# First conditioned product ahead of the third merge group, its weights made in halves, x loaded by SyncE

## The chip, the cores and the metric

The kernel runs on one core of one Trainium2 chip. The metric is device time in microseconds of one execution, lower is better. Engines in this text: PE (TensorE), ACT (ScalarE), DVE (VectorE), POOL (GpSimd), SP (SyncE, which only issues DMAs here). Each takes its own instructions in order, and they wait for each other by semaphores.

## What is computed

The input x has 8 batches of 256 tokens of width 128 (2048 tokens). Two layers follow each other, each a conditioning step and a feed-forward network:

```python
# layer 0: conditioning, a two-layer net whose weights depend on the batch's id
hidden_i = x @ wi.T + 2 * (x @ common_wi_a.T) @ common_wi_b.T + expert_lora(x, ids, ...)
hidden_o = relu(hidden_i) @ wo.T + 2 * (...)          # the same low-rank terms for wo
# layer 0: mixture of 4 experts, top 2 by a gate, 4 rounds with residual
for r in range(4):
    logits = cur @ Wg[r] + bg[r]; top 2, softmax -> cw
    y = gelu(cur @ W1[e] + b1[e]) @ W2[e] + b2[e]      # all 4 experts
    cur = cur + sum_e cw[e] * y[e]
x = x + cur
# layer 1: language low-rank projection, then a gated net of ternary weights
x = x + ffn1(lora(x, language) + embedding)
```

`wi` is 512x128 and `wo` 128x512. With the low-rank terms added, each batch has its own two weight matrices of 128x512; the kernel calls them (b, 0) for the first and (b, 1) for the second.

## The kernel before

The tokens lie on the free axis in four chunks of 512 columns, two batches to a chunk, and the 128 features on the partitions. Every product of 32-bit numbers is made of three matmuls on parts rounded to fp32r: `product` (L503) multiplies the high part of the weights with the high part of x (L505) and with its low part (L506), and the low part of the weights with the high part of x (L509). So every operand is first split: a high part is a rounding copy, mostly on ACT, and a low part is operand minus high part, on DVE or POOL.

The change touches only the stretch ahead of the loop over the expert rounds. What happens there:

- **Loads.** SP issues ids, vectors, factors of batch 0, 2, 4, 5, 6, 7 (`first_load`, `lora_load`, `expert_load` at L247), then the expert weights `moe_w` in four loads of 512 KB into `cw_all` (`moe_raw`), then small language factors. ACT issues `cond_base` (wi and wo), chunk 0 of x, and the factors of batches 1 and 3. POOL issues chunks 1 to 3 of x (L413).
- **Merge groups** (`merge_group`, L511). Low-rank factors are multiplied into PSUM banks, seven groups in the order of `MERGE_GROUPS`: (b, 0) by one 512-column matmul (L524), (b, 1) by four of 128 columns (L527). `MERGE_BANKS` names the bank of each; a group waits until the sums out of its banks are done.
- **Sums, high and low parts of the merged weights.** DVE adds the base (`merged_sum`, L1025) in the order `SUMS`, ACT rounds (`merged_high`, L798, into `mer_hi`, shown as ffn_hi) in the order `HIGHS`, POOL subtracts (`merged_low`, L417, into `mer_lo`, shown as ffn_lo) in the order `LOWS`; only (0, 0) has its low part on DVE (`first_low`, L1030). Six buffers hold the sums, four batches the parts.
- **x.** `x0_high` (ACT, L876) and `x0_low` (DVE for chunks 0, 2, 3, POOL for 1) split the chunks.
- **cond_hidden(b)** (L552) is the first conditioned product of a batch, 4 x 3 matmuls of 256 columns; `relu_high` (ACT, L871) and `relu_low` (DVE, L1209) split its result. **cond_out(b)** (L572) is the second one, 12 matmuls into bank COND. After two batches `conditioned_high` and `conditioned_copy` (ACT, L880, L885) and `conditioned_low` (DVE, L1043) take the chunk out; the next cond_out waits for that.
- **moe_high** (ACT, L890) and **moe_low** (POOL, L428) split the expert weights piece by piece, the first gate and the first expert of the first chunk are begun (`expert_in`, four pieces), `merge_lang` (L540) makes the language weights, and the loop over the rounds begins.

`warm` (L587) issues matmuls of zeros: 13 at the start and `KEEP_WARM` = 2 behind the second merge group. The order on each engine is written out by hand, on PE in L673 to L706:

```python
            merge_group(0)
            merge_group(1)
            warm(KEEP_WARM)
            merge_group(2)
            merge_group(3)
            cond_hidden(0)
            cond_hidden(1)
            merge_group(4)
            cond_out(0)
```

In the text the groups are counted from one: the third group is `merge_group(2)`.

## Time and profile before

| what | us |
|---|---|
| median of 3 runs | 485.58 (485.28 to 486.13) |
| profiled execution, device time | 486.61 |
| its span, first to last instruction | 484.8 |
| PE busy | 477.9 (99%) |
| ACT busy | 393.9 (81%) |
| DVE busy | 387.7 (80%) |
| POOL busy | 118.7 (24%) |

The span is 1.8 us shorter than the profiled execution's own time, and that execution is 1.0 us above the median of the runs. A page row of a busy engine says nothing yet about where time is lost; for that one asks for the waits of the engine that is nearly always busy, and for its instructions in order of time. The stretch ahead of the loop is the first 45 us of the span.

### The profile page before, as it was taken

To read this page: it belongs to the slowest core of one execution; us is meant where nothing else is said; L and a number is where in the kernel's file an instruction comes from. 1 tells how busy PE (TensorE), PEld (TensorE's weight loads), DVE (VectorE), ACT (ScalarE), POOL (GpSimd) and SP (SyncE) were. 2 spreads that over 40 slices of the span, in tenths; PEclk is the share of its full clock that TensorE was granted. 3 is DMA by queue.
4 is the path that set the end of the run, shared out by engine and by line. 5 is a ranking of instruction groups with operands and counts; after the bars stand their busy time and mean duration, and the time that the engine had idled before them with its cause. 6 is when DMAs were issued, how large, how long until landed. Compare 5 with 4: busy or idle time off the path is not lost.

```text
span 484.8 us, 7478 instructions
## 1 busy us (share of the span) xinstructions
PE 477.9 (99%) x2270; PEld 397.0 (82%) x2270; DVE 387.7 (80%) x641; ACT 393.9 (81%) x542; POOL 118.7 (24%) x102
## 2 busy tenths in 40 slices
PE   7999999999999999999999999999999999999997
PEld 7998888888888888888888888888888887888885
DVE  4789899999879898988898898889897758554343
ACT  3799988888888888988888888888888888697653
POOL 5796212121212112121222121231313144400000
PEclk9999999999999999999999999999999999999999
DMA  7702702020201102020202012120202000000001
GB/s 209 215 5 88 266 18 89 2 87 3 87 11 76 71 16 87 0 87 0 87 0 87 11 76 82 49 89 0 87 2 87 2 0 0 1 0 1 0 22 69
DMA packets 6986, 26.30 MB, mean 54 GB/s; under 512 B 2226, under 2 KB 2610, under 8 KB 4786
## 3 DMA queue, kind: packets, MB, share of 16 engines
q1 hardware_dynamic: 5826, 21.20, 12.1%
q0 software_dynamic: 528, 3.67, 2.2%
q10 hardware_dynamic: 608, 1.11, 0.8%
q8 instruction: 14, 0.23, 0.2%
q14 instruction: 10, 0.08, 0.0%
HBM read 24.81 MB, written 1.18 MB: 54 GB/s over the span
## 4 chain that ended last, share of the span: by engine, by line
PE 96%; DMA 2%; SPq 1%; issue 0%; DVE 0%
PE bank L505 34%; PE bank L506 34%; PE bank L509 26%; DMA stage<-lora_all 2%; PE bank L594 1%; PE bank L595 1%; PE bank L527 1%; SPq L244 0%; SPq L247 0%; PE bank L540 0%; PE bank L524 0%; SPq L257 0%; DVE x L1276 0%; SPq L345 0%; SPq L344 0%
## 5 line engine op out<-in xcount | busy, mean ns | idle before, releaser
L812 ACT ACTIVATE act_out<-bank,vec 128x512 f32<-128x512 f32 x256 | 165.4, 682 | 41.8 <-PE bank L509 32.6
L1115 DVE TENSOR_TENSOR hid_lo<-act_out,hid_hi 128x1024 fp32r<-128x1024 f32 x128 | 156.6, 1243 | 33.3 <-ACT hid_hi L817 33.2
L817 ACT ACTIVATE hid_hi<-act_out 128x1024 fp32r<-128x1024 f32 x128 | 135.9, 1062 | 8.0 <-PE bank L509 0.2
L468 POOL TENSOR_TENSOR cur<-cur,prod 128x512 f32<-128x512 f32 x48 | 64.9, 1352 | 238.4 <-DVE prod L1126 237.9
L505 PE MATMUL bank<-hid_hi,moe_hi 128*128 128x512 f32 x256 | 99.9, 390 | 0.0
L509 PE MATMUL bank<-hid_hi,moe_lo 128*128 128x512 f32 x256 | 99.7, 390 | 0.0
L505 PE MATMUL bank<-xhi,moe_hi 128*128 128x512 f32 x256 | 99.7, 390 | 0.0
L506 PE MATMUL bank<-hid_lo,moe_hi 128*128 128x512 f32 x256 | 99.7, 389 | 0.0
L506 PE MATMUL bank<-xlo,moe_hi 128*128 128x512 f32 x256 | 99.6, 389 | 0.0
L509 PE MATMUL bank<-xhi,moe_lo 128*128 128x512 f32 x256 | 99.6, 389 | 0.0
L505 PEld LDWEIGHTS bank<-hid_hi,moe_hi 128*128 128x128 f32 x256 | 48.1, 188 | 11.3 <-issue 0.2
L509 PEld LDWEIGHTS bank<-hid_hi,moe_lo 128*128 128x128 f32 x256 | 48.1, 188 | 10.2
L506 PEld LDWEIGHTS bank<-hid_lo,moe_hi 128*128 128x128 f32 x256 | 48.1, 188 | 10.1
L509 PEld LDWEIGHTS bank<-xhi,moe_lo 128*128 128x128 f32 x256 | 48.1, 188 | 10.0
L505 PEld LDWEIGHTS bank<-xhi,moe_hi 128*128 128x128 f32 x256 | 48.0, 188 | 10.0
L506 PEld LDWEIGHTS bank<-xlo,moe_hi 128*128 128x128 f32 x256 | 48.1, 188 | 9.9
L1126 DVE SCALAR_TENSOR_TENSOR prod<-bank,vec,cw_all 128x512 f32<-128x512 f32 x64 | 47.5, 742 | 0.2 <-PE bank L509 0.2
L505 PE MATMUL bank<-hid_hi,ffn_hi 128*128 128x512 f32 (+1 forms) x108 | 37.8, 353 | 0.0
L506 PE MATMUL bank<-hid_lo,ffn_hi 128*128 128x512 f32 (+1 forms) x108 | 37.4, 350 | 0.0
L999 ACT ACTIVATE act_out<-bank,vec 128x512 f32<-128x512 f32 x32 | 21.3, 685 | 14.5 <-PE bank L506 14.3
L505 PE MATMUL bank<-xhi,ffn_hi 128*128 128x512 f32 (+1 forms) x84 | 30.4, 362 | 0.0
L506 PE MATMUL bank<-xlo,ffn_hi 128*128 128x512 f32 (+1 forms) x84 | 30.0, 357 | 0.0
(126 smaller groups left out, 569.9 us busy)
## 6 DMA issues: line engine op xcount, KB each, us to landing
cw_all<-cw_dram SPq DMA_DIRECT2D x16, 1024.0 KB, 4.6
stage<-ffn_w POOLq DMA_DIRECT2D x1, 2304.0 KB, 8.5
cw_all<-moe_w SPq DMA_DIRECT2D x4, 512.0 KB, 10.3
stage<-lora_all SPq DMA_DIRECT2D x5, 160.0 KB, 7.1
x<-x_t POOLq DMA_DIRECT2D x3, 256.0 KB, 7.0
out_t<-x SPq DMA_DIRECT2D x3, 256.0 KB, 2.5
cur<-cond_base ACTq DMA_DIRECT2D x2, 256.0 KB, 3.1
stage<-ffn_w POOLq DMA_DIRECT2D x1, 512.0 KB, 3.8
```

What stands on the lines that cost most here:

```text
L468: pool.tensor_tensor(cur[:, c, :], cur[:, c, :], prod[:, s % 2, :], ALU.add).then_inc(add_done, 1)
L505: pe.matmul(out, w_hi, r_hi, start=start, stop=False)
L506: mm = pe.matmul(out, w_hi, r_lo, start=False, stop=stop and w_lo is None)
L509: return pe.matmul(out, w_lo, r_hi, start=False, stop=stop)
L527: mm = pe.matmul(bank[:, at, fc * D:(fc + 1) * D], factors[:, fc * P:(fc + 1) * P], factors[:, F:F + D], start=True, stop=True)
L594: pe.matmul(bank[0:SQ, at, :], wg_now[:], xhi[:, c, :], start=True, stop=False)
L595: pe.matmul(bank[0:SQ, at, :], wg_now[:], xlo[:, c, :], start=False, stop=True).then_inc(logit_done, 1)
L812: act.activation(act_out[:, f // 2, f % 2, :], bank[:, f, :], ACT.Gelu_apprx_tanh, bias=vec[:, V_B1 + e * FC + f:V_B1 + e * FC + f + 1]).t ...
L817: act.activation(hid_hi[:, s % 2, 2 * pr:2 * pr + 2, :], act_out[:, pr, :, :], ACT.Copy)\
L999: act.activation(act_out[:, o // 2, o % 2, :], bank[:, o + FC * (at % 2), :], ACT.Gelu, scale=vec[:, v + o:v + o + 1]).then_inc(gelu_done, 1)
L1115: dve.tensor_tensor(hid_lo[:, s % 2, 2 * pr:2 * pr + 2, :], act_out[:, pr, :, :], hid_hi[:, s % 2, 2 * pr:2 * pr + 2, :].bitcast(F32), ALU ...
L1126: dve.scalar_tensor_tensor(prod[:, s % 2, :], bank[:, 4 + s % 2, :], vec[:, V_B2 + e:V_B2 + e + 1], cw_all[:, c % 2, e, :], ALU.add, ALU.m ...
```

## The change

On PE, cond_hidden(0) moves from behind the fourth merge group to directly behind the second one and its warming matmuls, of which there are now three. The weights (0, 0) that it needs are summed, rounded and subtracted in two halves of 256 columns (`first_sum`, `first_merged_high`, `first_low`), with semaphores of their own, and PE waits for the second half before the third piece of the product. The third and fourth group write banks 6, 7, 4, 5 instead of 2, 3, 6, 7. Chunks 1 to 3 of x are issued by SP: chunk 1 behind the factors of batch 2, chunks 2 and 3 behind those of batch 7 and ahead of the expert weights. x0_low(2) and the low parts of conditioned chunks 2 and 3 go from DVE to POOL, where the latter read the copy in `cur` instead of the bank, so that cond_out(6) waits for the copy alone. The split of the gate weights goes from DVE to POOL. The orders of sums, high and low parts, and the lists of ACT, DVE and POOL up to the loop are rewritten; cond_hidden(4) moves behind cond_out(2).

```diff
-MERGE_BANKS = (6, 7, 4, 5, 2, 3, 6, 7, 5, 6, 7, 5, 6, 7, 5, 6)
+MERGE_BANKS = (6, 7, 4, 5, 6, 7, 4, 5, 5, 6, 7, 5, 6, 7, 5, 6)
-WARM, KEEP_WARM = 13, 2
+WARM, KEEP_WARM = 13, 3
...
             expert_load(sp, 2, expert)
+            x_load(sp, 1)
             for b in (4, 5, 6, 7):
                 lora_load(sp, b)
+            x_load(sp, 2)
+            x_load(sp, 3)
...
-            pool.wait_ge(first_out_in[1], 16)
-            for c in range(1, CHUNKS):
-                x_load(pool, c)
...
+            def conditioned_low(c):
+                pool.wait_ge(cond_cur, c + 1)
+                pool.tensor_tensor(xlo[:, c, :], cur[:, c, :], xhi[:, c, :].bitcast(F32), ALU.subtract)\
+                    .then_inc(xs_done, 1)
...
+            split_gate()
             merged_low(1, 0)
             merged_low(0, 1)
+            merged_low(1, 1)
             x0_low(1)
-            merged_low(1, 1)
...
                 for f in range(FC):
+                    if b == 0 and f % 2 == 0:
+                        pe.wait_ge(first_lo_done, f // 2 + 1)
...
+                elif b == PER_CHUNK * (CHUNKS - 1):
+                    pe.wait_ge(cond_cur, c)
...
             warm(KEEP_WARM)
+            cond_hidden(0)
             merge_group(2)
             merge_group(3)
-            cond_hidden(0)
...
-            cond_hidden(4)
             merge_group(6)
             cond_out(2)
+            cond_hidden(4)
             cond_out(3)
...
+            def first_merged_high():
+
+                for half, summed, done in zip(halves, (first_sum_done, merge_free), (first_hi_done, mer_hi_done)):
+                    act.wait_ge(summed, 1)
+                    act.activation(mer_hi[:, 0, 0, half], merged(0, 0)[:, half], ACT.Copy).then_inc(done, 1)
...
             base_load(act, 1)
+            x0_high(0)
             lora_load(act, 3)
-            x0_high(0)
-            merged_high(0, 0)
+            first_merged_high()
...
+            def first_sum():
+
+                dve.wait_ge(base_in[0], 16)
+                dve.wait_ge(merge_done, MERGED.index((0, 0)) + 1)
+                for half, summed in zip(halves, (first_sum_done, merge_free)):
+                    dve.scalar_tensor_tensor(merged(0, 0)[:, half], bank[:, merge_bank(MERGED.index((0, 0))), half], COND_ALPHA,
+                                             base[:, 0, half], ALU.mult, ALU.add).then_inc(summed, 1)
...
-            split_gate()
             x0_low(0)
-            merged_sum(0, 0)
+            first_sum()
+            first_low()
             merged_sum(1, 0)
             merged_sum(0, 1)
-            first_low()
```

On ACT, between the first relu and the first conditioned step, before. ffn_hi is a high part of merged weights, `hid_hi<-bank` a relu, `xhi<-x` a chunk of x, `xhi<-bank` the conditioned chunk's high part, `moe_hi` an expert piece.

```order
L871 ACTIVATE hid_hi<-bank 128x1024
L798 ACTIVATE ffn_hi<-stage 128x512
L798 ACTIVATE ffn_hi<-act_out 128x512
L876 ACTIVATE xhi<-x 128x512
L871 ACTIVATE hid_hi<-bank 128x1024
L798 ACTIVATE ffn_hi<-stage 128x512
L880 ACTIVATE xhi<-bank 128x512
L876 ACTIVATE xhi<-x 128x512
L885 ACTIVATE cur<-bank 128x512
L890 ACTIVATE moe_hi<-cw_all 128x512
```

The same place after the change, from the second relu to the copy of the conditioned chunk.

```order
L903 ACTIVATE hid_hi<-bank 128x1024
L922 ACTIVATE moe_hi<-cw_all 128x512
L824 ACTIVATE ffn_hi<-fifth 128x512
L908 ACTIVATE xhi<-x 128x512
L903 ACTIVATE hid_hi<-bank 128x1024
L824 ACTIVATE ffn_hi<-stage 128x512 x2
L912 ACTIVATE xhi<-bank 128x512
L917 ACTIVATE cur<-bank 128x512
```

The first expert piece stood behind the first conditioned chunk's copy and now stands ahead of it, behind relu_high(1).

On SP, from the factors of batch 7 on, before: the expert weights follow at once.

```order
L244 TENSOR_LOAD ids
L244 ISA x2
L247 ISA
L247 DMA stage<-lora_all 64x640
L355 DMA cw_all<-moe_w 128x1024 x4
```

And after, with the last two chunks of x between them (chunk 1 stands in the same way behind the factors of batch 2).

```order
L247 TENSOR_LOAD ids
L247 ISA x2
L250 ISA
L250 DMA stage<-lora_all 64x640
L265 DMA x<-x_t 128x512 x2
L361 DMA cw_all<-moe_w 128x1024 x4
```

Three x loads, one of them further ahead, now stand before the first load of expert weights.

## Rows read from the trace of the kernel before

**Rows 1.** The page, part 1: busy us (share) and instructions.

```profile
PE 477.9 (99%) x2270; PEld 397.0 (82%) x2270; DVE 387.7 (80%) x641; ACT 393.9 (81%) x542; POOL 118.7 (24%) x102
```

**Rows 2.** Waits of PE, whole span: us in total, times, longest.

```profile
PE bank L524 <- DMA stage<-lora_all: 2.3, 2, 1.8
```

**Rows 3.** PE in order of time: start, us, instruction [idle before, releaser].

```profile
9.53 0.70 PE L524 MATMUL bank<-stage 32*128 32x512 f32 x2 [1.78 <-DMA stage<-lora_all]
...
10.74 0.38 PE L505 MATMUL bank<-xhi,ffn_hi 128*128 128x256 f32 x1
...
15.90 0.70 PE L524 MATMUL bank<-stage 32*128 32x512 f32 x2 [0.53 <-DMA stage<-lora_all]
...
17.00 0.38 PE L505 MATMUL bank<-hid_hi,ffn_hi 128*128 128x256 f32 x1
...
22.68 0.28 PE L505 MATMUL bank<-xhi,ffn_hi 128*128 128x256 f32 x1
...
24.12 0.28 PE L505 MATMUL bank<-xhi,ffn_hi 128*128 128x256 f32 x1
...
26.74 0.38 PE L505 MATMUL bank<-hid_hi,ffn_hi 128*128 128x256 f32 x1
...
44.02 0.50 PE L505 MATMUL bank<-xhi,moe_hi 128*128 128x512 f32 x1
```

**Rows 4.** Three stretches: us, busy by engine, PE clock, DMA share, GB/s.

```profile
7.67:11.08 3.41, 1.62 (x23) 1.46 (x23) 2.74 (x5) 2.42 (x4) 2.29 (x3) 1.00 0.82 236
11.08:14.49 3.41, 3.41 (x19) 3.41 (x18) 2.06 (x4) 1.68 (x3) 1.81 (x2) 0.50 1.03 263
14.49:17.90 3.41, 2.88 (x26) 2.58 (x26) 2.10 (x3) 2.59 (x5) 2.63 (x3) 1.00 1.03 336
```

**Rows 5.** DVE in order of time: first sums, first low part, a 256-column operation.

```profile
6.91 1.29 DVE L1025 SCALAR_TENSOR_TENSOR prod<-bank,cur 128x512 f32<-128x512 f32 x2
...
8.71 0.68 DVE L1030 TENSOR_TENSOR ffn_lo<-prod,ffn_hi 128x512 fp32r<-128x512 f32 x1
...
34.28 0.41 DVE L1065 TENSOR_TENSOR bank<-bank,logit 32x256 f32<-32x256 f32 x1
```

**Rows 6.** ACT in order of time: an expert piece, a relu, a high part.

```profile
24.38 0.63 ACT L890 ACTIVATE moe_hi<-cw_all 128x512 fp32r<-128x512 f32 x1
24.90 1.02 ACT L871 ACTIVATE hid_hi<-bank 128x1024 fp32r<-128x1024 f32 x1
25.80 0.64 ACT L798 ACTIVATE ffn_hi<-fifth 128x512 fp32r<-128x512 f32 x1
```

**Rows 7.** SP's issues in order of time.

```profile
4.75 5.55 SPq L247 DMA_DIRECT2D stage<-lora_all  x5
10.34 2.21 SPq L355 DMA_DIRECT2D cw_all<-moe_w  x4
```

**Rows 8.** DMA issues near 1.2, 4.7, 5.8, 10.3: size, us to landing.

```profile
x<-x_t ACTq DMA_DIRECT2D x1, 256.0 KB, 3.2
...
stage<-lora_all SPq DMA_DIRECT2D x1, 160.0 KB, 3.8
...
x<-x_t POOLq DMA_DIRECT2D x1, 256.0 KB, 6.8
...
cw_all<-moe_w SPq DMA_DIRECT2D x1, 512.0 KB, 9.1
stage<-lora_all SPq DMA_DIRECT2D x1, 160.0 KB, 7.1
```

**Rows 9.** Stretches of 2 us, columns as in rows 4.

```profile
12.00:14.00 2.00, 2.00 (x11) 2.00 (x11) 1.14 (x2) 1.19 (x2) 0.64 (x1) 0.50 1.03 233
...
16.00:18.00 2.00, 2.00 (x20) 1.88 (x21) 0.97 (x2) 1.18 (x3) 1.12 (x1) 1.00 1.01 381
...
20.00:22.00 2.00, 2.00 (x21) 1.82 (x20) 1.61 (x3) 1.54 (x2) 2.00 (x3) 1.00 0.32 75
```

**Rows 10.** POOL in order of time: six expert low parts.

```profile
36.61 7.55 POOL L428 TENSOR_TENSOR moe_lo<-cw_all,moe_hi 128x512 fp32r<-128x512 f32 x6
```

More of the change, by code:

```diff
@@ L454, in _ @@
             moe_low(3)
+            conditioned_low(2)
+            pool.wait_ge(cond_cur, CHUNKS)
+            for i in range(2):
+                pool.memset(prod[:, i, 0:1], 0.0).then_inc(add_done, 1)
             moe_low(7)
+            conditioned_low(3)
             def mixture_add(rnd, s, last):
@@ L929, in _ @@
             merged_high(5, 1)
+            relu_high(5)
+            merged_high(7, 1)
             merged_high(6, 1)
[L931 to L935 removed]
+            moe_high(6)
             relu_high(6)
+            moe_high(3)
             conditioned_high(2)
```

130 lines of the change are left out of this document (61 added, 69 removed).

## The prediction

> **What bounds the kernel now.** I read the page's busy times first, then the waits of the tensor engine, then its order of time with the clock of each stretch, and last what feeds that stretch. The tensor engine (PE) is busy for 477.9 of 484.8 us [rows 1], and over the whole span, once it has begun, it waits only for low-rank factors that a DMA brings: twice, 2.3 us in total, 1.8 us of it before the third merge group at 9.53 [rows 2, 3]. After 15.90 it never waits for another engine again. One more loss is no wait: the granted clock is 0.50 (1.2 GHz) from 11.08 to 14.49, after a stretch in which PE was busy 1.62 of 3.41 us, and 1.00 (2.4 GHz) before and after [rows 4]. The first conditioned product, whose 12 matmuls take 1.44 us at the full clock (22.68 to 24.12, the same block for batch 3), lies in that stretch. So all that the change can win lies ahead of 16 us: 2.3 us of waits and about 1.6 us of slow clock, 3.9 us together; from 16 us on PE has only to be kept fed. A gain there reaches the end one for one, since PE works without a wait from there.
>
> **The first product, moved ahead of groups 3 and 4.** Today the row at 10.74 is cond_hidden(0) [rows 3]. Its weights are a chain: the sum on VectorE (DVE) from 6.91, the high part on ScalarE (ACT), the low part on DVE from 8.71, 0.68 us [rows 5], and two other sums stand between. After the change the chain is made in halves with nothing between. A half has 256 columns; its price on each engine lies between the 0.41 us of a 32x256 operation and the 0.68 us of the whole [rows 5]; I take 0.41, since length along the row is what both have in common, for each of three steps. The first half is summed from 6.9 as now, and 6.9 + 3 x 0.41 + 0.1 for handovers gives 8.2: the first product starts 2.5 us earlier. Even at 0.68 each it starts at 9.0. The second half follows 0.3 us later and PE needs it 0.7 us later, so it costs nothing. The third warming matmul fills time in which PE would stand still. If the clock holds, the product ends at 9.7, groups 3 and 4 follow (1.21 us today, 9.53 to 10.74) and are now held by the sums of group 2, because their banks are 6, 7, 4, 5 again: three more sums at the 0.6 us at which sums follow each other come behind the halves, so (1,1) is done at 10.3 and the groups end at about 11.1, not 10.9: 0.2 us, which the wait before cond_out(0) would take anyway. Their own factors, of batch 3 above all, are issued 0.6 us later by ACT, behind x0_high(0); today the wait for them ends at 9.53, so they are due at 10.1 at the latest, 0.4 us after the product; I count 0.1, since x is not yet under way on a second queue.
>
> **Up to cond_out(2).** cond_hidden(1) ends near 12.7. The fifth group's factors (batch 5) are issued at 7.9, 0.55 later than now; today that wait ends at 15.90, some 8.5 us after the issue, while the first factors of this size from SP land after 3.8 us [rows 8]: 11.7 to 16.4. I take 12 to 13, because x chunks 2 and 3 are no longer ahead of them; past 14 each us would be lost. The group then ends near 13.9. cond_out(0) needs the low part of the first hidden block. relu_high(0) now stands behind x0_high(1) and the high part of (2,0), whose sum waits for group 3 and ends at 11.5: it starts at 12.1, takes 1.0, and after sums (2,0), (3,1), (3,0), (2,1), ending at 13.2, DVE's relu_low(0) ends at 14.4. So cond_out(0) starts at 14.6; today it starts at 17.00. Four products at 1.44 to 1.5 and two merge groups at the 1.10 us of 15.90 to 17.00 follow, 8.1 us: PE could start cond_out(2) at 22.7. Today it starts it at 26.74, after one product more (cond_hidden(4), 1.44). This is the floor.
>
> **What is late next: the expert weights.** cond_out(2) overwrites the bank that the first conditioned chunk sits in, so it waits for conditioned_low(0) on DVE, which waits for two ACT steps. ACT takes its work in order, and its new list has moe_high(0) ahead of merged_high(4,0), x0_high(3), relu_high(2), merged_high(4,1), merged_high(5,0) and those two steps. moe_high(0) waits for the first piece of moe_w. Call its landing M. From M: six 512-column steps at 0.52 (24.38 to 24.90), one relu at 0.90 (24.90 to 25.80) make 4.0 us up to and with the first conditioned step, the copy 0.6 (a step alone takes 0.63), the DVE low part 0.68, handovers 0.2 [rows 6]: cond_out(2) cannot start before M + 5.47. From there to the last block ahead of the loop (expert_in piece 3, at 44.02) PE needs today's 44.02 - 26.74 = 17.28 us and the 1.44 us of cond_hidden(4), which now stands behind. So that block starts at **M + 24.19**, and the break-even with today is M = 19.83.
>
> **Where M lands.** Today the first moe load is issued at 10.34 and lands 9.1 us later, at 19.4; the factors of batch 7, issued ahead of it at 9.8 (the last of the five), land after 7.1 us, at 16.9 [rows 7, 8]. Moving x from GpSimd's queue (POOL) to SyncE's (SP) puts three more issues ahead of the moe loads, 0.55 us each as the moe loads' own are (2.21 for four): the first moe issue moves to 12.0. Upper bound: the same 9.1 us from issue, M = 21.1. Lower bound: x chunk 3, issued at 11.45, lands in the 3.2 us of the first x load, 14.65, and 0.52 MB follow at 381 GB/s in 1.4 us, M = 16.0. Between them: the four factor loads and three x loads are 1.44 MB, which at the mixed stretch's 233 GB/s [rows 9] from 8.5 (4.75 + 3.8, when the load ahead of them has landed) end at 14.7; SP issues factors only every 1.27 us (five in 5.55) while 0.16 MB take 0.7, so its queue runs dry for perhaps 0.8 in all, 15.5; and today moe lands 2.5 us after the last load ahead of it. **M = 18.0.** I take this since it uses how the same queue behaves at the same place. The last block then starts at 42.19 against 44.02, 1.83 us earlier. Its own x landings: chunk 1 is issued at 5.35 and lands between 8.55 (3.2 us) and 12.15 (6.8, today's time on the other queue) [rows 8]; it delays relu_high(0) from 10.4 on, and I take 9.5, since it has only one factor load ahead. Chunk 2 (10.9, between 14.1 and 17.7) holds relu_high(1) and would decide from 15.2 on; I take 14.6.
>
> **POOL and DVE.** POOL gets x0_low(2) and conditioned_low(2), (3), three operations like those of its moe_lo row, six in 7.55 us [rows 10]: 3 x 1.26 = 3.8 us, and the small gate split before 6 us, when it idles. It loses the three x issues. Today its last low part ends at 44.2. After, low parts that PE needs come in time: merged_low(7,1), the tightest, ends at about 37.5 and cond_out(7) wants it at 38.9. POOL then ends near 45.4, and only loads and additions that the loop wants after 50 wait for it. Cost 0, and the cover is 1.4 us thick; beyond that every us counts. conditioned_low from DVE saves it 2 x 0.68 where it was not late. Other edits cost nothing: PE's second wait inside the first product is met as shown, and logits for chunk 1 ahead of cond_out(5), and the products of chunk 3 exchanged with pieces of the first expert, are the same matmuls in another order.
>
> **Sum** against the profiled execution: 486.61 (span 484.8 and 1.8 around it) less 1.83 is 484.8. The same difference taken from the median of the runs, 485.58, gives 483.75, so **483.8**.
>
> **Rivals.**
>
> (a) The DMA engines are the bound and the order of issue changes nothing. They are at 1.03 of full share from 12 to 14 and 1.01 from 16 to 18 [rows 9], and the bytes ahead of the first moe piece are the same in both kernels. Then M stays 19.4: the last block at 43.6, 0.4 us saved, 485.1. Against it: in the mixed stretch they move 233 GB/s at the share at which they move 381 later, so the share is not bytes. A late x chunk 1 (12.15, which gives 1.75 us back) or late factors of batch 5 (16.4) end close to it and are counted here.
>
> (b) The last load's tail goes away. After 20 us the engines are at 0.32 of their share, 75 GB/s [rows 9], though moe is still landing: a few of the 16 lag. If GpSimd's x loads cause that, moe follows x chunk 3 evenly, M is 16.9, and the floor of 22.7 decides: 22.7 + 18.72 = 41.4, 2.6 saved, 483.0. The Trainium skill (DMA: Bandwidth & Descriptors, section "Latency and other measured facts") says that two of the sixteen are usually slower and guesses that the descriptor rings of GpSimd's queue cause it; the trace shows the lag, not its cause.
>
> (c) The clock falls again. Instead of one pause of 1.8 us there are several: about 0.3 at 8, 0.2 at 12.7, 0.6 at 13.9, 0.8 at 22.7. Today a pause of 0.5 us left the clock at 1.00 (14.49 to 17.90, PE busy 2.88 of 3.41), one of 1.8 us brought 0.50 [rows 4]. A stretch at 0.50 costs up to 1.6 us, some of it inside pauses; I count 1.4: 485.2. The Trainium skill (TensorE: Matmul & The Clock Gate, section "A second HAM failure mode: psum-queue depth-cycling") warns of just this, short pauses between groups of matmuls that cycle through PSUM banks, which speaks against four groups on four banks; by that rule this case, with 485.2, would be the likeliest, by the row of the 0.5 us pause it is not.
>
> (d) Slower. The moe loads keep their 9.1 us from issue because SP's single queue is what delays them, and now it also carries x. M = 21.1, last block at 45.3, 1.3 later: **486.9**. It is slower than before from M = 19.8, measurably from 20.8.
>
> **How the numbers follow.** Forecast (M from 17 to 18.8, no slow stretch): 0.40; (a) 0.24; (b) 0.12; (c) 0.12; (d) 0.12. About 0.2%, 0.97 us, is what a measurement can tell here. Faster by more: the forecast and (b), 0.52; within: (a) and (c), 0.36; slower: (d), 0.12. The range goes from the floor with 0.1 to spare, 482.9, to 486.2: it takes in the forecast, (a), (b), (c) and the half of (d) with M up to 20.5.
>
> **What would show it.** First product at 8.2 to 8.6 in the order of time; no wait of PE for a DMA; a wait of about 0.8 us before cond_out(2), put down to DVE's conditioned low part, and before it ACT waiting for cw_all<-moe_w until 18; clock 1.00 from 7.67 to the end; last block at 42.2. I am wrong if ACT waits for moe_w to 19.4 or beyond, if a window shows 0.50, if cond_out or cond_hidden waits on POOL's ffn_lo, or if the loop, which nothing here touches, takes longer than now.

## The result, and the profile after the change

The changed kernel takes 487.24 us (median of 14 executions, 486.05 to 489.12) against 485.38 us (14 executions, 484.39 to 486.28) of the kernel before, measured on one chip. The ratio is 1.0045, with a 95% interval of 1.0034 to 1.0056. The kernel is slower by 0.45%; the forecast was 483.8 with a range of 482.9 to 486.2, and the measured time lies above it.

The profiled execution took 487.13 us, its span is 485.3. The page's busy times, which answer [rows 1]:

```profile
PE 477.5 (98%) x2272; PEld 395.9 (82%) x2272; DVE 387.4 (80%) x636; ACT 394.0 (81%) x543; POOL 121.0 (25%) x106
```

PE does the same work. What changed is where it waits. Waits of PE over the whole span, after (engine, bank and line, released by: total us, times, longest), to be held against [rows 2]:

```profile
PE bank L529 <- DVE xlo L1084: 1.7, 1, 1.7
PE bank L616 <- POOL blank L408: 1.1, 1, 1.1
PE bank L529 <- issue: 0.6, 1, 0.6
PE bank L548 <- DMA stage<-lora_all: 0.5, 2, 0.3
PE bank L529 <- DVE ffn_lo L1071: 0.2, 1, 0.2
```

The 2.3 us for factors [rows 2] have shrunk to 0.5. (The 1.1 us is the start, before anything can run.) In their place stand 1.7 us for DVE's low part of the first conditioned chunk and 0.8 us in two other places. PE in order of time, after, with the columns of [rows 3]:

```profile
8.95 0.36 PE L529 MATMUL bank<-xhi,ffn_hi 128*128 128x256 f32 x1 [0.20 <-DVE ffn_lo L1071]
...
10.84 0.70 PE L548 MATMUL bank<-stage 32*128 32x512 f32 x2 [0.23 <-DMA stage<-lora_all]
...
15.69 0.36 PE L529 MATMUL bank<-hid_hi,ffn_hi 128*128 128x256 f32 x1 [0.61 <-issue]
...
25.70 0.36 PE L529 MATMUL bank<-hid_hi,ffn_hi 128*128 128x256 f32 x1 [1.66 <-DVE xlo L1084]
...
44.31 0.50 PE L529 MATMUL bank<-xhi,moe_hi 128*128 128x512 f32 x1
```

These are the first product, the third group, cond_out(0), cond_out(2) and the last block ahead of the loop. That block starts at 44.31, and 44.02 before [rows 3], though the stretch at half clock of [rows 4] is absent. Who holds cond_out(2) is seen on ACT, after:

```profile
20.17 0.63 ACT L922 ACTIVATE moe_hi<-cw_all 128x512 fp32r<-128x512 f32 x1 [2.75 <-DMA cw_all<-moe_w]
20.71 0.62 ACT L824 ACTIVATE ffn_hi<-fifth 128x512 fp32r<-128x512 f32 x1
21.23 0.61 ACT L908 ACTIVATE xhi<-x 128x512 fp32r<-128x512 f32 x1
21.75 1.01 ACT L903 ACTIVATE hid_hi<-bank 128x1024 fp32r<-128x1024 f32 x1
22.66 1.14 ACT L824 ACTIVATE ffn_hi<-stage 128x512 fp32r<-128x512 f32 x2
23.69 0.58 ACT L912 ACTIVATE xhi<-bank 128x512 fp32r<-128x512 f32 x1
24.17 0.59 ACT L917 ACTIVATE cur<-bank 128x512 f32<-128x512 f32 x1
```

ACT stands still for 2.75 us until the first piece of expert weights is there. Then it works through six steps and the copy without a gap; DVE takes the low part at 24.87, and PE goes on at 25.70. SP's issue of those weights, to be held against [rows 7], and its size and time to landing, against [rows 8]:

```profile
12.02 2.72 SPq L361 DMA_DIRECT2D cw_all<-moe_w  x4
```

```profile
cw_all<-moe_w SPq DMA_DIRECT2D x1, 512.0 KB, 8.1
```

12.02 + 8.1 is 20.1: this is M, forecast at 18.0. The stretches of 2 us that answer [rows 9] (us, busy by engine, PE clock, DMA share, GB/s):

```profile
12.00:14.00 2.00, 1.86 (x19) 1.57 (x15) 2.00 (x4) 1.30 (x2) 2.00 (x2) 1.00 0.70 171
14.00:16.00 2.00, 1.39 (x15) 1.23 (x15) 2.00 (x3) 1.91 (x5) 2.00 (x3) 1.00 0.91 237
16.00:18.00 2.00, 2.00 (x19) 2.00 (x18) 1.95 (x4) 1.43 (x2) 2.00 (x3) 1.00 0.98 229
18.00:20.00 2.00, 2.00 (x20) 1.75 (x19) 0.76 (x2) 0.00 (x0) 2.00 (x2) 1.00 1.01 377
```

From 12 to 14 the DMA engines are at 0.70 of their share and move 171 GB/s, where before they were at 1.03 and 233 [rows 9]. From 16 to 18 their share is 0.98, but they move 229 GB/s where they moved 381 before; 377 comes only after 18. Everything from 45 us on is as it was: PE is busy without a gap from 45 to 400 in both kernels.

The clock needs one more look. In the profiled execution it is 1.00 throughout the first 45 us. But each timed execution lists its mean granted clock, and in 6 of these 14 it is 0.996, in the others 0.999 or 1.000. One stretch of 3.41 us at 0.50, as in [rows 4], lowers the mean over 485 us by 0.5 x 3.41 / 485 = 0.0035, about this much. The 6 took 488.04 to 489.12, the other 8 took 486.05 to 487.34. The execution of the kernel before from which the prediction was made was itself one at 0.996 (486.61 us), and such executions are rare in that kernel: 2 of the 119 timed in the experiments below. So at full clock the changed kernel needs 486.98 (median of the 8) and the kernel before about 485.2; the rest, 0.26 us of the median, comes with the clock.

### The profile page after: what moved, and what is told of

Its sections match the earlier page's. It is cut to its first block, busy times and chain, and to the rows that moved or that the text cites. A ratio compares the mean times of both kernels' runs of the same rounds, so it can differ in the third digit from the quotient of the medians.

```text
span 485.3 us, 7483 instructions
## 1 busy us (share of the span) xinstructions
PE 477.5 (98%) x2272; PEld 395.9 (82%) x2272; DVE 387.4 (80%) x636; ACT 394.0 (81%) x543; POOL 121.0 (25%) x106
## 4 chain that ended last, share of the span: by engine, by line
PE 94%; SPq 2%; DMA 2%; ACT 1%; issue 1%; DVE 0%; ACTq 0%; DVEq 0%
PE bank L529 34%; PE bank L530 33%; PE bank L533 25%; DMA cw_all<-moe_w 2%; PE bank L620 1%; PE bank L621 1%; SPq L247 1%; SPq L250 1%; SPq L265 0%; ACT ffn_hi L824 0%; PE bank L564 0%; ACT hid_hi L903 0%; SPq L260 0%; DVE xlo L1084 0%; ACT cur L917 0%
## 5 line engine op out<-in xcount | busy, mean ns | idle before, releaser
L844 ACT ACTIVATE act_out<-bank,vec 128x512 f32<-128x512 f32 x256 | 165.3, 682 | 42.7 <-PE bank L533 33.7
L1156 DVE TENSOR_TENSOR hid_lo<-act_out,hid_hi 128x1024 fp32r<-128x1024 f32 x128 | 158.8, 1260 | 31.9 <-ACT hid_hi L849 31.8
```

The source lines that it names most:

```text
L844: act.activation(act_out[:, f // 2, f % 2, :], bank[:, f, :], ACT.Gelu_apprx_tanh, bias=vec[:, V_B1 + e * FC + f:V_B1 + e * FC + f + 1]).t ...
L1156: dve.tensor_tensor(hid_lo[:, s % 2, 2 * pr:2 * pr + 2, :], act_out[:, pr, :, :], hid_hi[:, s % 2, 2 * pr:2 * pr + 2, :].bitcast(F32), ALU ...
```

## Experiments

Several things are new at once: the place of moe_high(0) on ACT's list, the x loads on SP's queue with the later expert weights, and the early first product with its lists and banks. My theory after the profile was that the first two together cost the time, because the list meets a load that is not there; the rivals were that the early product, x on SP alone, or the new lists cost it. The first four kernels were compared on one chip with 485.05 us (27 executions) of the kernel before.

**The changed kernel again**, for a second profile.

> The changed kernel itself, as the measure for the others on the same chip. Theory A (the first load of expert weights lands at 20.1 and ACT's list makes all wait for it): ratio to before near 1.0045, PE waits about 1.7 us for DVE's conditioned low part before cond_out(2), last block ahead of the loop near 44.3. Theory B (the clock decides: the changed kernel falls to 0.50 in some executions and then costs 1.5 us more): runs with a mean clock of 1.000 near 486.7, runs with 0.996 near 488.5, and the median between them depends on how many of each there are.

487.14 us (6 executions), ratio 1.0045 [1.0029, 1.0061]. The picture repeats: M is 20.05, cond_out(2) at 25.58 after a wait for the same low part. What differs is the start: the first merge group begins at 6.81 and not at 6.23, and the first product 0.58 later too:

```profile
9.53 0.36 PE L529 MATMUL bank<-xhi,ffn_hi 128*128 128x256 f32 x1 [0.68 <-DVE ffn_lo L1071]
...
25.58 0.36 PE L529 MATMUL bank<-hid_hi,ffn_hi 128*128 128x256 f32 x1 [1.23 <-DVE xlo L1084]
```

The start-up's 0.58 us is taken back by a shorter wait before cond_out(2), since that wait ends with M. Two of the 6 executions show a mean clock of 0.996, and they are the longest (488.13 and 488.16); the other four have a median of 486.83.

**moe_high(0) later.** The one edit is the place on ACT's list.

```diff
             relu_high(1)
-            moe_high(0)
             merged_high(4, 0)
...
             conditioned_copy(0)
+            moe_high(0)
             moe_high(4)
```

> One edit in the changed kernel: on ACT, moe_high(0) stands behind conditioned_copy(0), as it did before the change, instead of behind relu_high(1). Theory A: ACT no longer waits for cw_all<-moe_w before the first conditioned chunk, the wait of PE before cond_out(2) goes from 1.7 us to at most 0.2, the last block starts near 42.6, and the median falls by 1.7 us, to 485.5, ratio 1.000. Theory B: the wait goes, but the time still falls in two groups 1.5 us apart; a median of 486.5 or more would speak for B. A rival to both, that the engines have simply more to do in this order: the wait moves to cond_out(4) or to the low parts and the median stays at 487.2.

485.87 us (12 executions), ratio 1.0014 [1.0004, 1.0025]. 1.3 us come back, about six tenths of the loss. The weights land at 19.8 (12.03 + 7.8), but nobody waits. PE's waits up to 46 us in this kernel, beside the start:

```profile
PE bank L529 <- issue: 0.6, 1, 0.6
PE bank L548 <- DMA stage<-lora_all: 0.4, 1, 0.4
PE bank L529 <- DVE ffn_lo L1071: 0.2, 1, 0.2
```

The 1.7 us are gone, and so are the executions at 0.996: none of these 12, none of 10 in the repetition below, against 8 of 20 of the changed kernel. So about 1.0 of the 1.3 us is the wait (486.83 less 485.87), and the rest comes with the clock. cond_out(2) and the last block ahead of the loop start at:

```profile
23.83 0.38 PE L529 MATMUL bank<-hid_hi,ffn_hi 128*128 128x256 f32 x1
...
42.46 0.50 PE L529 MATMUL bank<-xhi,moe_hi 128*128 128x512 f32 x1
```

No wait stands before this cond_out(2). 23.83 is where PE itself comes to it; the prediction's floor had 22.7.

**The load earlier instead.** The place stays, the first load of expert weights is issued ahead of x chunks 2 and 3.

```diff
-            x_load(sp, 2)
-            x_load(sp, 3)
             for i in (0, 2, 1, 3):
                 half = slice((i % 2) * 2 * F, (i % 2 + 1) * 2 * F)
                 sp.dma_start(moe_raw[:, i // 2, half], moe_w[:, i // 2, half]).then_inc(moe_in[i], 16)
+                if i == 0:
+                    x_load(sp, 2)
+                    x_load(sp, 3)
```

> One edit in the changed kernel: SP issues the first load of expert weights ahead of x chunks 2 and 3, not behind them. Theory A with its formula (last block at landing + 24.2): the first load is issued at 10.9 instead of 12.0 and has 512 KB less ahead of it, so it lands near 18 and the last block would start near 42.4 by it; but x chunk 2 lands about 1.5 us later (near 17), and relu_high(1) stands behind it, which gives 43.5 to 44.0 (landing + 27). Median 486.0 to 486.7. If the landing does not move (DMA engines full, order of issue without effect), the time stays at 487.2.

485.95 us (10 executions), ratio 1.0021 [1.0011, 1.0031]. The first piece is issued at 10.92 and lands 4.2 us later, at 15.1, and moe_high(0) runs at 18.64, directly behind relu_high(1), without waiting:

```profile
18.64 0.62 ACT L923 ACTIVATE moe_hi<-cw_all 128x512 fp32r<-128x512 f32 x1
```

```profile
cw_all<-moe_w SPq DMA_DIRECT2D x1, 512.0 KB, 4.2
```

Its last block starts at 43.27, after waits of 0.68, 0.31 and 0.61 us ahead of 17. Two independent ways of taking away the meeting of place and landing give the same 1.2 to 1.3 us. That the meeting costs this much, with the clock that comes with it, is shown. That neither comes back to 485.1 shows that there is a second, smaller cost.

**The early first product alone**, in the kernel before: cond_hidden(0) ahead of the third group, the weights in halves, three warming matmuls; banks, loads and all other lists as before.

```diff
-WARM, KEEP_WARM = 13, 2
+WARM, KEEP_WARM = 13, 3
...
             warm(KEEP_WARM)
+            cond_hidden(0)
             merge_group(2)
             merge_group(3)
-            cond_hidden(0)
...
-            merged_sum(0, 0)
+            first_sum()
+            first_low()
             merged_sum(1, 0)
             merged_sum(0, 1)
-            first_low()
```

> The kernel before with one part of the change alone: cond_hidden(0) directly behind the second merge group, its weights made in halves, three warming matmuls; loads, banks and all other orders as before. Theory A: what ends the first 16 us is the landing of batch 5's factors (15.75), not the product before it and not the slow clock, which is hidden in that wait. So PE's wait for factors at the fifth group grows from 0.5 to 1.0 to 2.2 us and the time stays at before's: 485.4, ratio 0.999 to 1.001. The rival, which the prediction's upper bound of 3.9 us took for granted (pauses and slow clock ahead of 16 us add up): 1.5 to 3 us faster, 482.5 to 484.

485.61 us (11 executions), ratio 1.0010 [1.0001, 1.0019]. It gains nothing. The wait for the factors of batch 5, which I expected to grow, is not there either. PE in order of time:

```profile
9.30 0.36 PE L508 MATMUL bank<-xhi,ffn_hi 128*128 128x256 f32 x1 [0.68 <-DVE ffn_lo L1048]
...
13.49 0.36 PE L508 MATMUL bank<-xhi,ffn_hi 128*128 128x256 f32 x1 [1.42 <-POOL ffn_lo L420]
```

The first product starts 1.4 us earlier than its 10.74 of [rows 3], no factor is waited for any more, and 1.42 us are waited before cond_hidden(1). The profile puts that down to POOL, but the operation of POOL that ends there (13.35) is the low part of (0, 1), which this product does not read; its own, of (1, 0), ended at 12.1. DVE's list names the other candidate:

```profile
12.05 0.69 DVE L1034 SCALAR_TENSOR_TENSOR fifth<-bank,cur 128x512 f32<-128x512 f32 x1 [0.77 <-PE bank L530]
12.66 0.68 DVE L1034 SCALAR_TENSOR_TENSOR act_out<-bank,cur 128x512 f32<-128x512 f32 x1
```

These are the sums of (2, 0) and (3, 0), out of banks 2 and 3, and the second ends at 13.34. cond_hidden(1) writes banks 2 and 3, so it waits for both. The old order hid this: groups 3 and 4 and a whole product lay between. So the product can't be moved without new banks for the third group; the third and fourth group on banks 6, 7, 4, 5, as in the change, are what the move needs, and what it costs shows in four_moves below. What is saved at 9.5 is waited at 13.5.

**The kernel before again**, since its first profile was the odd one.

> The kernel before once more, for a profile of an execution with a mean clock of 1.000 (27 timed executions of it so far: 26 at 0.998 to 1.000 with a span of 482.2 to 484.4, one at 0.996 with 484.8, like the one profiled first). Theory C: the profile that the prediction was made from is the rare case. The common one has no stretch at 0.50 and its last block ahead of the loop starts near 42.5, not at 44.02, so that the changed kernel's 44.3 is 1.8 us late against it. If C falls, this profile again shows 44.0 and a stretch at 0.50, and the 1.5 us are elsewhere.

485.04 us (8 executions) against 485.09 (26) of the same kernel, ratio 0.9995 [0.9985, 1.0005]. Its profile:

```profile
9.53 0.70 PE L524 MATMUL bank<-stage 32*128 32x512 f32 x2 [1.23 <-DMA stage<-lora_all]
...
14.76 0.70 PE L524 MATMUL bank<-stage 32*128 32x512 f32 x2 [0.89 <-DMA stage<-lora_all]
...
42.89 0.50 PE L505 MATMUL bank<-xhi,moe_hi 128*128 128x512 f32 x1
```

No stretch at 0.50, and the last block at 42.89 and not at 44.02. The pause at 9.53 is 1.23 us here and was 1.78 in [rows 3], where the half clock followed. The expert weights land 7.5 us after their issue at 10.30, at 17.8.

**x by SP, alone**, in the kernel before: the three x loads move to the places that they have after the change.

```diff
             expert_load(sp, 2, expert)
+            x_load(sp, 1)
             for b in (4, 5, 6, 7):
                 lora_load(sp, b)
+            x_load(sp, 2)
+            x_load(sp, 3)
...
-            pool.wait_ge(first_out_in[1], 16)
-            for c in range(1, CHUNKS):
-                x_load(pool, c)
```

> The kernel before with the loads of the change alone: x chunks 1 to 3 by SP, as in the changed kernel; all lists as before. In the old list of ACT the first expert piece stands behind the first conditioned chunk's copy (24.4), where even a landing at 20.1 delays nothing. Theory A: no loss from the late expert weights, and the factors of batch 5 land at 12 instead of 14 to 16: 0 to 0.7 us faster, 484.4 to 485.1. If putting x into SP's queue is harmful as such, it is slower by 0.5 us or more and the cause is not ACT's list alone.

485.29 us (12 executions), ratio 1.0004 [0.9993, 1.0014]: nothing. The expert weights are issued at 12.02 and land 8.3 us later, at 20.3, as in the changed kernel, and it costs nothing, because moe_high(0) stands behind the copy in this list. So the late landing by itself is harmless. This profile shows the half clock of [rows 4] once more, behind a pause of 1.52 us at 9.83 (columns as there):

```profile
7.67:11.08 3.41, 1.89 (x26) 1.61 (x25) 2.67 (x6) 2.65 (x5) 1.91 (x2) 1.00 0.73 219
11.08:14.49 3.41, 3.41 (x20) 3.41 (x19) 2.37 (x4) 1.21 (x2) 3.40 (x3) 0.57 0.59 169
```

Three of its 12 executions are at 0.996, and they are the three longest (486.25 to 487.13).

**The new lists with x by POOL again**: the changed kernel with the edit above undone.

> The changed kernel with the loads of before: x chunks 1 to 3 by POOL again, the new lists kept. The first expert load is issued at 10.4 again and by theory A lands at 19.4 or earlier, 0.7 us sooner; but x chunk 1 lands near 12.6, and relu_high(0) now stands behind x0_high(1) on ACT: the model of the lists gives a last block near 45.0 for that, 488. So A expects 487.5 to 488.5, slower than the changed kernel. If what makes the changed kernel slow is the load order as such, this one is faster than it, 485.5 to 486.5.

487.14 us (7 executions), ratio 1.0040 [1.0025, 1.0055]. Taking x off SP's queue does not mend the changed kernel. moe_high(0) runs at 18.08, but x chunk 1 now holds ACT until 12.09 and the factors of batch 5 hold PE. Its waits:

```profile
PE bank L548 <- DMA stage<-lora_all: 1.7, 1, 1.7
...
PE bank L529 <- POOL ffn_lo L432: 0.7, 2, 0.5
PE bank L529 <- issue: 0.6, 1, 0.6
```

This time is equal to that of the changed kernel and lies below the 487.5 that I expected, but it is made of other waits, and the last block starts at 44.61; without the profile one would have read it as "the loads have no effect". These waits suggest that the new lists need x early, and that the move to SP brings them about what the late expert weights then take; how much of each was not measured apart.

**moe_high(0) early, alone**, in the kernel before.

```diff
             relu_high(1)
+            moe_high(0)
             merged_high(4, 0)
...
             conditioned_copy(0)
-            moe_high(0)
```

> The kernel before the change with one edit: moe_high(0) stands behind relu_high(1) on ACT's list, as in the changed kernel; the loads are as before, so that its load lands near 18 to 19.4 instead of 20.1. Theory (the harm is the place and the late landing together): cond_out(2) waits for M + 5.3 at most, 23.2 to 24.7, which is ahead of the 25.2 at which PE comes there, so no wait appears before it; the high parts of (4,0) and (3,0) move back by up to 1.8 us and may cost cond_hidden(3) up to 0.6; time 485.1 to 485.8. Rival (the place alone costs it, wherever the load lands): a wait of a microsecond or more before cond_out(2) or cond_hidden(3), 486.4 or more.

486.45 us (10 executions), ratio 1.0023 [1.0013, 1.0032] to 485.22 (27) of before. The time is the rival's, and the theory's was too low: the place costs 1.2 us even with the loads where they were. In the profiled execution the weights landed at 17.0 (10.32 + 6.7), earlier than in the three profiles of the kernel before, and no wait stands before cond_out(2), as the theory had it. The cost sits one product earlier:

```profile
23.10 0.39 PE L505 MATMUL bank<-xhi,ffn_hi 128*128 128x256 f32 x1 [0.62 <-POOL ffn_lo L417]
```

ACT's high parts of (4, 0) and (3, 0) come later, POOL's low parts after them, and cond_hidden(3) waits. With a landing at 17.8 to 19.4, as in the three profiles of the kernel before, this wait would be longer by as much; that this makes up the 1.2 us of the median is likely, but only the 0.62 is shown.

**moe_high(0) later, with four more moves**, the attempt to beat both kernels. The edits to the kernel of moe_high_later:

```diff
-LOWS = ((1, 0), (0, 1), (1, 1), (2, 0), (2, 1), ...
+LOWS = ((1, 0), (0, 1), (2, 0), (1, 1), (2, 1), ...
...
-            merged_low(1, 1)
             x0_low(1)
             merged_low(2, 0)
+            merged_low(1, 1)
...
-            x0_high(0)
             lora_load(act, 3)
+            x0_high(0)
...
-            merged_high(2, 0)
             relu_high(0)
+            merged_high(2, 0)
...
-            merged_sum(2, 1)
             relu_low(0)
+            merged_sum(2, 1)
```

> The changed kernel with moe_high(0) behind conditioned_copy(0) (as in moe_high_later) and four small moves: lora_load(3) ahead of x0_high(0) as before the change, relu_high(0) ahead of merged_high(2,0) on ACT, relu_low(0) ahead of merged_sum(2,1) on DVE, x0_low(1) and merged_low(2,0) ahead of merged_low(1,1) on POOL. Theory (what is left of the gap to the kernel before is the wait of 0.55 us before cond_out(0) and the 0.2 us at the third group): in the profile cond_out(0) starts directly behind the fifth group, near 14.8 instead of 15.35, no new wait up to the loop, last block ahead of the loop 0.5 to 0.7 earlier than the 42.3 of moe_high_later, time 485.87 less 0.6 = 485.3, at or just above the kernel before. Rival (the extra comes from elsewhere, from the landings that vary from execution to execution, or from a later wait that takes the place): the wait before cond_out(0) is gone in the profile and the time stays at 485.7 to 486.0.

486.01 us (11 executions), ratio 1.0010 [1.0001, 1.0019]. The rival's time; the theory's profile did not come either. The wait before cond_out(0) is still there, with another releaser:

```profile
15.12 0.35 PE L529 MATMUL bank<-hid_hi,ffn_hi 128*128 128x256 f32 x1 [0.70 <-DVE prod L1057]
```

And DVE in order of time in the same kernel:

```profile
11.23 0.69 DVE L1057 SCALAR_TENSOR_TENSOR fifth<-bank,cur 128x512 f32<-128x512 f32 x1 [0.76 <-PE bank L548]
...
13.15 1.23 DVE L1237 SCALAR_TENSOR_TENSOR hid_lo<-bank,hid_hi 128x1024 fp32r<-128x1024 f32 x1
14.29 0.68 DVE L1057 SCALAR_TENSOR_TENSOR prod<-bank,cur 128x512 f32<-128x512 f32 x1
```

relu_low(0) now ends at 14.4, but the sum of (2, 1), moved behind it, ends at 15.0, and cond_out(0) starts at 15.12. The code shows the reason, a bank: cond_out writes bank COND, which is 4, and MERGE_BANKS of the change puts (2, 1) into bank 4, so `pe.wait_ge(merge_free, summed_in(COND, ...))` waits for that sum. Before the change (2, 1) is in bank 6, and only (0, 1) has to be out of bank 4. So after the change cond_out(0) stands behind four sums and the low part of the relu on DVE in either order, 4 x 0.6 + 1.2 = 3.6 us from 11.23 on. This is a cost of the new bank order that I had not seen.

**moe_high(0) later once more**, for a second profile.

> moe_high_later once more, for a second profile and more timed executions. Theory (its profile at 485.04 was one of its shortest executions and its usual one is 0.8 us longer by waits for DMAs that vary): the median stays at 485.6 to 486.0, and this profile shows, beside the 0.55 us before cond_out(0), a longer wait for factors, or warming matmuls that end later. Rival (the first comparison was off and the kernel equals the one before): median 484.9 to 485.3.

485.93 us (10 executions), ratio 1.0012 [1.0003, 1.0021], so the remaining loss of 0.6 to 0.7 us is real. PE in order of time:

```profile
9.27 0.36 PE L529 MATMUL bank<-xhi,ffn_hi 128*128 128x256 f32 x1 [0.26 <-DVE ffn_lo L1071]
11.25 0.70 PE L548 MATMUL bank<-stage 32*128 32x512 f32 x2 [0.31 <-DVE stage L1057]
14.32 0.70 PE L548 MATMUL bank<-stage 32*128 32x512 f32 x2 [0.17 <-DVE prod L1057]
16.09 0.36 PE L529 MATMUL bank<-hid_hi,ffn_hi 128*128 128x256 f32 x1 [0.61 <-issue]
```

Again the first group began late (6.54), and the first product and everything behind it with it; the last block is at 43.00 against 42.46 in the first profile of this kernel. The fifth group waits 0.17 us for DVE's sum of (3, 0), out of bank 7. At the third group the profile names a sum of DVE too, but the one that ends at 11.25 is (1, 1), and this group needs only (1, 0), which ended at 10.06. What it waits for is the factors of batch 3: ACT issues them at 6.48, behind x0_high(0), and they land 4.6 us later, at 11.1. In moe_load_earlier it is the same, 6.28 + 5.1 = 11.4 with the group at 11.52. In four_moves they are issued at 5.01, and no wait stands there.

**Factors first**, in the kernel before: is there something to win at 9.5 at all?

```diff
-            base_load(act, 1)
             lora_load(act, 3)
+            base_load(act, 1)
```

> The kernel before the change with one edit: ACT issues the factors of batch 3 ahead of the second half of cond_base, not behind it (about 0.5 us earlier; those of batch 2, by SP at 4.7, stay). Theory (what the kernel before can still win is its wait for factors ahead of the third group, and a gain there reaches the end): the wait at 9.53 ends at 8.8 to 9.1, then by batch 2's factors (4.72 plus 3.9 is 8.6), the last block ahead of the loop and the time come 0.3 to 0.6 us earlier, 484.6 to 484.9, unless the wait before the fifth group grows by the same. Rival (the wait before the fifth group, 0.89 at 14.76 in before_again, ends with a load that does not move, so what is saved at 9.5 is waited there): the first wait is shorter, the second longer by the same, time 485.2 as before. Second rival: wo lands later and the sum of (0,1) waits for it, which moves the fourth chain back: 485.4 or more.

485.78 us (12 executions), ratio 1.0005 [0.9995, 1.0014] to 485.18 (23). No gain. The wait for factors does fall, to 0.45 us with the third group at 8.64, and the first product waits for DVE instead:

```profile
8.64 0.70 PE L524 MATMUL bank<-stage 32*128 32x512 f32 x2 [0.45 <-DMA stage<-lora_all]
11.51 0.39 PE L505 MATMUL bank<-xhi,ffn_hi 128*128 128x256 f32 x1 [1.40 <-DVE ffn_lo L1030]
```

DVE had waited 0.27 us for wo until 9.17, ahead of the low part, which is the second rival, and that low part took 1.68 us in this execution, 0.68 in [rows 5]. The larger part of the 1.40 us is thus this one long operation, and a single profile does not say how much of the median it makes.

**The kernel before, a third profile.**

> The kernel before the change once more, for a third profile. Theory (the third group starts at 9.5 whenever the first one starts, since it waits for factors, so the start-up, which varied from 5.57 to 6.82 in the profiles, is covered there): first merge group anywhere from 5.6 to 6.8, third group at 9.2 to 9.6, last block ahead of the loop at 42.2 to 42.9, and last block minus third group minus later waits near 32.5. In the changed kernel the first product follows the first group 2.7 us later whenever it starts, so a late start goes to the end. Rival: the third group moves with the first one here too.

485.20 us (8 executions), ratio 1.0000 [0.9990, 1.0010]. Its profile:

```profile
9.50 0.70 PE L524 MATMUL bank<-stage 32*128 32x512 f32 x2 [0.55 <-DMA stage<-lora_all]
15.73 0.36 PE L505 MATMUL bank<-hid_hi,ffn_hi 128*128 128x256 f32 x1 [0.78 <-issue]
42.94 0.50 PE L505 MATMUL bank<-xhi,moe_hi 128*128 128x512 f32 x1
```

In the three profiles of this kernel the first group starts at 5.67, 6.16 and 6.14, and the third at 9.53, 9.53 and 9.50. In five of the changed order (the changed kernel, changed_again, both of moe_high_later, four_moves) the first group starts at 6.23, 6.81, 6.16, 6.54 and 5.77 and the first product at 8.95, 9.53, 8.88, 9.27 and 8.49, always 2.72 or 2.73 us behind it. The rival (the third group moves along here too) has little room: the groups were only 0.5 apart.

## Why the prediction failed, point by point

Three steps failed: the landing M of the first expert piece (18.0, measured 20.1), the last block of the kernel before against which the sum was taken (44.02, typically 42.9), and the floor, the time at which PE itself comes to cond_out(2) (22.7, measured 24.0).

**The chain behind M was right.** The two formulas in M hold. M + 5.47 is 25.6 (measured 25.70), and M + 24.19 is 44.3 (44.31). ACT's list with moe_high(0) in it is what ends last, and ACT waits for moe_w beyond 19.4, which the prediction had named as a sign of being wrong.

**M was mis-sized**: 18.0 forecast, 20.1 measured, 20.05 in the second profile. The issue at 12.0 was right (12.02), and so was the step that the weights land 2.5 us after the last load ahead of them: x chunk 3, issued at 11.54, lands 6.3 us later, at 17.8, and M comes 2.3 behind. Wrong was that this load lands at 15.5. I had the four factor loads and three x loads end there, "its queue runs dry for perhaps 0.8 in all". The queue ran drier: the DMA share is 0.70 from 12 to 14, with 171 GB/s and not 233. And what moved was not only what stands ahead in the list: from 8.5 to 17.8 the windows of 2 us add up to about 1.9 MB (my estimate from their rates), while those seven loads are 1.44 MB and the factors of batch 3 0.16. So some 0.3 MB of the expert weights probably moved before the last x chunk had landed. The landing took 8.1 us from the issue, 7.4 to 8.3 in the six profiles with these loads, and 6.2 to 9.1 in seven profiles with the loads of before. Rival (d)'s rule, the load keeps its time from issue, was nearer than bytes over rate: with 6.2 to 9.1 it gives 18.2 to 21.1. I gave it 0.12. It is no law either: in moe_load_earlier the same load, issued 1.1 us earlier and ahead of two x loads, landed after 4.2 us, 5 us earlier than in the changed kernel. The two x loads, 0.52 MB, cost it 3.9 us beside their own issue time, where 1.4 us would do at 381 GB/s. So what a queue does with the loads around this one was priced too low; no run was made to tell whether they are served in turn or side by side. Rival (a), the engines as the bound and M at 19.4, is not what happened: from 12 to 14 they stood at 0.70 of their share. Rival (d)'s time of 486.9 is near the measured 487.2, but by luck: it has M at 21.1, a microsecond too late, and the same baseline, a microsecond too late as well.

**The baseline was the second failure.** The sum set M + 24.19 against 44.02, the last block of an execution with a stretch at half clock; in the two other profiles of the kernel before that block starts at 42.9. I then took the difference off the median of the runs, 485.58. The 3.9 us that the prediction called all that can be won held 1.6 us of slow clock which nearly no execution has. Against 42.9 the break-even is M = 18.7 and not 19.83. By this the measured M gives 1.4 us more, which with the 0.26 us of the clock is most of the 1.86 us measured; against 44.02 it would have given 0.3 us, a time inside the range. The forecast of M = 18.0 would have given 0.7 us less by the formula, not 1.83. The warning was there: the profiled execution was 1.0 us above the median, and its mean clock was 0.996.

**The floor was the third.** By the formula M = 18.0 has cond_out(2) at 23.47, but PE comes to it only at 24.04 in the changed kernel (25.70 less the wait of 1.66), and at 23.83 and 24.36 in the two profiles of moe_high_later, not at 22.7. So even with the landing as forecast PE's own start would have decided, and the last block would have come at about 42.7 (24.04 and the 18.61 from there to the last block), 0.2 us ahead of the kernel before, which is less than can be told here. moe_high_later, where M no longer counts, is not faster than the kernel before.

**"A gain there reaches the end one for one" is false at 9.5 us.** first_product_alone and factors_first take the wait for factors away or shorten it, and both get another one, 1.42 us for sums out of banks 2 and 3 and 1.40 us for DVE's low part, and neither is faster. The factors, the sums on DVE and POOL's low parts arrive close to each other there. That PE never waits after 15.90 I had taken as a proof that only feeding it earlier was needed.

**The first product** starts at 8.95, 9.53 in the second profile, not at 8.2. Each step in halves took 0.38 (0.76 for two), close to the 0.41 taken; but the sum started at 7.47 and not at 6.9, since it follows the first group, which varied from 5.57 to 6.82 over the profiles. Before the change, that variation ended in the wait for factors; now the first product follows it, and in the versions without the wait before cond_out(2) so does the last block (42.23, 42.46 and 43.00 for first groups at 5.77, 6.16 and 6.54).

**Up to cond_out(2).** The fifth group was forecast to end near 13.9 and starts at 13.91, 1.1 us late, though batch 5's factors were there in time. cond_out(0) was forecast at 14.6 and starts at 15.69: the first product came 0.75 later, the third group waited 0.23 more, and four sums plus relu_low(0) follow on DVE. The effect on the end in the changed kernel is none, since M decides; in moe_high_later it counts. The wait at the third group has the forecast's size (0.2, measured 0.23) but not its cause: I had put it down to DVE's sums, and it is the factors of batch 3, issued at 6.38 behind x0_high(0) and landed 4.3 us later, for which I had counted 0.1. POOL at cost 0 came as said: no PE wait on POOL in either profile of the changed kernel.

**The clock.** Rival (c) had it that several short pauses bring the half clock. In moe_high_later all the short pauses are there (0.15 to 0.61 us) and no long one, and none of 22 executions has a mean clock of 0.996. With the 1.2 to 1.7 us before cond_out(2) in addition, 8 of 20 have. By the rule of the Trainium skill (TensorE: Matmul & The Clock Gate, section "A second HAM failure mode: psum-queue depth-cycling") the short ones would be the danger; this case does not bear that out. No profile caught an execution of the changed kernel with the half clock, so that it follows this pause is inferred from the counts, not seen. A long pause alone does not settle it: first_product_alone has one of 1.42 us and none of 11.

**The tail.** Rival (b), that the last load's tail goes away with GpSimd's loads, did not come: from 22 to 24 the DMA engines are at 0.45 of their share.

```profile
22.00:24.00 2.00, 2.00 (x24) 1.72 (x23) 1.21 (x1) 2.00 (x4) 1.34 (x2) 1.00 0.45 127
```

The fourth load of expert weights landed 11.0 us after its issue, though GpSimd issued no load at all in the first 30 us of this kernel. The guess in the Trainium skill (DMA: Bandwidth & Descriptors, section "Latency and other measured facts"), that descriptor rings of GpSimd's queue slow two of the sixteen engines, is thus not supported as the cause of this tail; which engines lag was not looked at.

**What stays open.** moe_high_later is 0.12 to 0.14% (0.6 to 0.8 us) slower than the kernel before in two comparisons. Candidates that the profiles show are the first product that follows the start-up, the wait for batch 3's factors at the third group (0.31) and for a sum at the fifth (0.17), and bank 4. Another is a slightly longer chain on PE: from the first product to the last block, less the waits between, it is 33.03 and 32.64 us in its two profiles, and the same blocks, counted from the third group, took 32.47 and 32.66 in the two undisturbed profiles of the kernel before. How much each has of the 0.7 us was not separated, and the last blocks of the two kernels (42.46 and 43.00 against 42.89 and 42.94) lie too near to each other to show it in single executions. No version here beats the kernel before.

## What to carry to other kernels

A piece on an in-order list that waits for a DMA delays all that stands behind it, so give a moved piece a place at which even the latest landing measured in that queue is in time; a landing worked out from bytes and a rate was 2 us short here. A change that feeds the busiest engine earlier gains only if all that feeds it arrives earlier: list the second and third latest arrivals at the wait before counting the wait as gain. And look at the clock and time of the profiled execution first; if it is not like the median of the runs, take the differences against a typical one.

## What the runs showed of the hardware

- Whether a pause brings the half clock differs from execution to execution. Pauses of PE of 1.78 us (the first profile of before) and 1.52 us (loads_alone) were followed by a stretch at 1.2 GHz (the granted clock is 0.50 from 11.08 to 14.49 in the first, 0.50 from 12 to 14 in the second); pauses of 1.66 us (changed), 1.70 us (lists_with_pool_loads) and 1.42 us (first_product_alone) were not in their profiled executions. Over the timed ones, 8 of 20 of the changed kernel had a mean clock of 0.996, 3 of 12 of loads_alone, 1 of 7 of lists_with_pool_loads, none of 11 of first_product_alone, and 2 of 119 of the kernel before, whose pause at 9.5 us was 1.78, 1.23 and 0.55 us in its three profiles. An execution of the changed kernel with it took 1.7 us longer (median 488.65 against 486.98 in the first comparison).
- How long a load of 512 KB takes from its issue depends on its neighbours: 7.4 to 8.3 us behind two x loads in the same queue (six profiles), 4.2 us ahead of them (one), 6.2 to 9.1 us with x on another queue (seven), and 11.0 us for the fourth of a row.
- The same DVE subtraction of 128x512 took 0.68 us in [rows 5] and 1.68 us in factors_first. What stretched it was not tried.
